# A four-part transformer block: the first attention unit's transposes and position biases moved into the end of the first feed-forward network, and raw weights loaded ahead of rows

## What is computed

```python
x = x + attn_a(layernorm(x))   # a stack: 512 -> 64, 4 layers of long convolution and MLP, -> 512 (+ bout)
x = x + ffn(layernorm(x))      # (silu(x Wg) * (x Wu)) Wd, inner size 1792
x = x + attn_b(layernorm(x))   # 32 query heads, 8 key heads of 128, rms norm of q and k
x = x + ffn(layernorm(x))      # the same weights again

# attn_b, per sequence
scores = einsum(q, k) / sqrt(128)
rel = pos[None, :] - pos[:, None]
bias = where(rel > 0, -1e30, slope[head] * rel)
out = softmax(scores + bias) @ v
return out @ Wo.T
```

## Time and profile before

| | us |
|---|---|
| median of 3 runs (lowest, highest) | 2420.01 (2417.81, 2420.99) |
| the profiled execution | 2419.45 |
| its span | 2418.1 |
| PE busy | 2356.0 (97%) |
| DVE, ACT, POOL busy | 1590.2, 1204.3, 838.7 |
| mean granted clock of PE | 0.987 |

### The profile page before, as it was taken

One profiled execution on the slowest core, in us unless ns is written; L12 is line 12 of the kernel. 1 busy time (PEld: TensorE's weight loads), 2 busy tenths in 40 slices (PEclk: granted clock), 3 DMA queues, 4 the chain that ended last, 5 costly groups with the idle time before them and its releaser, 6 DMA issues.

```text
span 2418.1 us, 41023 instructions
## 1 busy us (share of the span) xinstructions
PE 2356.0 (97%) x12810; PEld 2028.0 (84%) x12810; DVE 1590.2 (66%) x3897; ACT 1204.3 (50%) x3788; POOL 838.7 (35%) x1332
## 2 busy tenths in 40 slices
PE   6899999999999999999999999999999999999999
PEld 4577777888888888989989999899899978888887
DVE  7666565534267777777777777677777776565553
ACT  6433332333256666666666666666666662232211
POOL 4540343211034345545444455454444440011000
PEclk7899999999999999999999999999999999999999
DMA  4334558987831534545446345444462315565554
GB/s 130 114 112 177 204 207 277 346 337 278 337 123 57 231 125 164 214 151 176 176 177 233 125 164 214 151 173 179 177 233 92 114 38 216 196 217 184 192 190 157
DMA packets 92629, 444.87 MB, mean 184 GB/s; under 512 B 10168, under 2 KB 17336, under 8 KB 72704
## 3 DMA queue, kind: packets, MB, share of 16 engines
q1 hardware_dynamic: 91056, 440.78, 49.4%
q10 hardware_dynamic: 1360, 1.46, 0.2%
HBM read 342.59 MB, written 99.61 MB: 183 GB/s over the span
## 4 chain that ended last, share of the span: by engine, by line
PE 84%; DMA 6%; issue 3%; ACT 3%; DVE 2%; POOL 1%; SPq 1%; ACTq 0%; DVEq 0%; POOLq 0%
PE psum L800 71%; DMA stage<-in_wqkv 3%; PE psum L2666 3%; PE psum L2642 2%; DMA weff_s<-short_st 1%; PE psum L2660 1%; PE psum L1811 1%; ACT prob L2408 1%; PE psum L1832 1%; DMA weff_q<-q_parts 1%; PE psum L1802 1%; PE psum L1844 1%; PE psum L2661 1%; POOL srstd L1202 1%; POOL prob L2471 1%
## 5 line engine op out<-in xcount | busy, mean ns | idle before, releaser
L800 PE MATMUL psum<-qw,xs 128*128 128x384 f32 x2688 | 548.1, 346 | 1.1 <-DVE su L2498 0.7
L800 PEld LDWEIGHTS psum<-qw,xs 128*128 128x128 f32 x2688 | 456.8, 188 | 2.5 <-issue 1.3
L2471 POOL TENSOR_SCALAR prob<-prob,rsum 128x128 f32<-128x128 f32 (+1 forms) x512 | 231.4, 465 | 529.1 <-DVE rsum L2574 528.0
L2408 ACT ACTIVATE prob<-biased,nmax 128x256 f32<-128x256 f32 (+1 forms) x512 | 226.9, 445 | 112.5 <-DVE nmax L2564 109.2
L2582 DVE TENSOR_TENSOR oT_l<-psum,oT_h 128x512 fp32r<-128x512 f32 x128 | 88.4, 691 | 196.0 <-ACT oT_h L2420 195.9
L800 PE MATMUL psum<-wo_h,oT_h 128*128 128x512 f32 x512 | 208.2, 407 | 0.0
L800 PE MATMUL psum<-wo_l,oT_h 128*128 128x512 f32 x512 | 202.9, 396 | 0.0
L800 PE MATMUL psum<-wo_h,oT_l 128*128 128x512 f32 x512 | 202.5, 395 | 0.0
L2354 ACT ACTIVATE squares<-cc 128x128 f32<-128x128 f32 x512 | 154.4, 305 | 45.6 <-DVE cc L2501 28.5
L2432 POOL TENSOR_TENSOR rr<-ss,mneg_half 128x6 f32<-128x6 f32 (+1 forms) x128 | 150.3, 1174 | 10.6
L2415 ACT ACTIVATE pT_h<-psum 128x384 fp32r<-128x384 f32 x256 | 124.8, 488 | 57.3 <-PE psum L2666 55.1
(11 more groups left out here) (339 smaller groups left out, 5939.0 us busy)
## 6 DMA issues: line engine op xcount, KB each, us to landing
xs<-weff_x SPq DMA_DIRECT2D x62, 1792.0 KB, 8.2
wgu<-weff_gu SPq DMA_DIRECT2D x42, 1024.0 KB, 7.5
qw<-weff_q SPq DMA_DIRECT2D x56, 768.0 KB, 7.5
weff_q<-q_parts SPq DMA_DIRECT2D x84, 384.0 KB, 4.9
wD<-weff_dn SPq DMA_DIRECT2D x56, 512.0 KB, 4.6
wS<-weff_s SPq DMA_DIRECT2D x28, 1024.0 KB, 6.8
wdn<-weff_dn SPq DMA_DIRECT2D x42, 512.0 KB, 4.2
weff_gu<-wgu SPq DMA_DIRECT2D x14, 1024.0 KB, 4.4
```

The lines of the kernel that those rows point to most:

```text
L800: ins = pe.matmul(out_ap, stat[a], mov[b], start=start and n == 0, stop=stop and n == last)
L2408: act.activation(prob[:, b, lo:hi], biased[:, b % 2, lo:hi], ACT.Exp, bias=nmax[:, b, t:t + 1], scale=-1.0, accum_out=esum[:, b, t:t + 1]) ...
L2471: pool.tensor_scalar(prob[:, b, lo:hi], prob[:, b, lo:hi], rsum[:, b, t:t + 1], 1.0, ALU.mult, ALU.mult).then_inc(prob_done, 1)
```

## The change

1. Unit 0's transposes go between `up` 55 and the downs, with ACT's and DVE's parts behind them; they use banks 6, 0 and 7 instead of 5, 4 and 6. The mask and the biases stand on DVE between `dlo` 54 and `d` 55, `rel` at the end of POOL's phase-1 list. ACT runs one exp of a single column there, so that its table is loaded.
2. PE no longer passes `phase1_over`. Scores of heads 2 and 3 and the first product of unit 1 wait for the x additions that free their banks.
3. SP loads the rows of units 1 and 2 as soon as `up` 55 is done.
4. In unit 0 the split of the output weights moves inside the unit (ACT after `exp1` and after `pThi1`; POOL after the second and after the fourth `prob`).
5. In every unit SP's order is `sets0 sets1 set0` instead of `sets0 set0 sets1`, and in `set0` `qf` stands ahead of `lx`.
6. The places `rows` and `set1` are earlier on PE, ACT and DVE, which moves steps in units 2 to 5 only.
7. POOL's `bout` of blocks 1 to 3 waits for the four `frow` of block 0, in the planner and on the chip.

```diff
@@ stack_steps
-                o.add(("bout", s, t), "pool", 1.27, [("fold", 5, 0), ("row", s, t), ("w1", 0, t) if lead else ("xadd", 0, 1)], 6)
+                o.add(("bout", s, t), "pool", 1.27, [("fold", 5, 0), ("row", s, t), ("w1", 0, t) if lead else ("frow", 0, TPB - 1)], 6)
@@ behind order1 = first.ordered(patient=PATIENT)
+        end = NBLK * IC - 1
+        def follows(engine, key, *steps):
+            at = order1[engine].index(key) + 1
+            order1[engine][at:at] = steps
+        follows("pe", ("up", end, 1), ("qT", 0, 0), ("kT", 0, 0), ("qT", 0, 1))
+        follows("act", ("dhi", end, 0), ("qThi", 0, 0), ("kThi", 0, 0), ("qThi", 0, 1), ("table", 0, 0))
+        follows("dve", ("dlo", end - 1, 0), ("mask", 0, 0), *(("alibi", 0, hd) for hd in range(GRP)))
+        follows("dve", ("dlo", end, 0), ("kw", 0, 0), ("qTlo", 0, 0), ("kTlo", 0, 0), ("qTlo", 0, 1))
+        order1["pool"].append(("rel", 0, 0))
@@ pool_phase1, bout
                     wait_stack_row(pool, a, b)
+                    if a:
+                        pool.wait_ge(row_done, TPB)
@@ act_phase1
+                elif what == "table":
+                    act.wait_ge(s_out, 32 * IC)
+                    act.activation(table[:], mneg_half[:, 0:1], ACT.Exp)
@@ UNIT_STEPS
-            "pe": "sc0 sc1 sc2 qkv1 qkv7 sc3 qkv6 pT0 qkv5 pT1 qkv2 qkv4 at0 pT2 pT3 qkv3 rows outa0 set1 qT0 at1 outa1 kT0 qT1 "
+            "pe": "sc0 sc1 sc2 qkv1 qkv7 sc3 qkv6 pT0 qkv5 pT1 qkv2 qkv4 at0 rows pT2 pT3 qkv3 set1 outa0 qT0 at1 outa1 kT0 qT1 "
...
-            "dve": "bias0 bias1 rsum0 bias2 rsum1 bias3 wait0 rsum2 u2 u3 pTlo0 c22 pTlo1 c11 rsum3 set0 u4 c21 oTlo0 pTlo2 c12 "
-                   "rows pTlo3 wait1 oTlo1 set1 qTlo0 qTlo1 kTlo0 oadd0 vlo0 oadd1",
-            "act": "set0 exp0 exp1 exp2 prcopy0 pThi0 exp3 pThi1 sqr5 sqr2 oThi0 pThi2 sqr4 pThi3 rows wait1 sqr3 ksc0 set1 oThi1 "
+            "dve": "bias0 bias1 rsum0 bias2 rsum1 bias3 wait0 rsum2 u2 u3 pTlo0 c22 pTlo1 c11 rsum3 set0 u4 c21 rows oTlo0 pTlo2 c12 "
+                   "pTlo3 wait1 oTlo1 set1 qTlo0 qTlo1 kTlo0 oadd0 vlo0 oadd1",
+            "act": "set0 exp0 exp1 swo0 exp2 prcopy0 pThi0 exp3 pThi1 swo1 sqr5 sqr2 oThi0 rows pThi2 sqr4 pThi3 set1 wait1 sqr3 ksc0 oThi1 "
...
-            "sp": "sets0 set0 sets1",
+            "sp": "sets0 sets1 set0",
@@ besides
+            if engine == "act" and b == 0 and (where in ("swo0", "swo1") if g == 0 else where == "set0"):
+                steps += [("swo", g, int(where[-1]))] if g == 0 else [("swo", g, 0), ("swo", g, 1)]
+            if engine == "pool" and b == 0 and where in (("wait0", "sums") if g == 0 else ("set0", "wait0")):
+                steps.append(("swo", g, (("wait0", "sums") if g == 0 else ("set0", "wait0")).index(where)))
...
+                if g and later_g < KVH and b == 1:
+                    steps.append(("qf", later_g, 0))
                 if u + 3 < UNITS and u + 3 not in range(SEQS1, BATCH):
                     steps.append(("lx", u + 3, 0))
-                if g and later_g < KVH and b == 1:
-                    steps.append(("qf", later_g, 0))
@@ sp_phase2, behind the load of qkw
+            sp.wait_ge(xs_out, 32 * SEQS1)
+            sp.wait_ge(up_mm, NBLK * IC)
+            load_rows(1)
+            load_rows(2)
             phase1_over(sp)
@@ pe_projection, product 1
                 pe.wait_ge(kT_lo, a)
+                if a == 1:
+                    pe.wait_ge(fx_done, NT)
@@ new: where the transposes go, and what they wait for in unit 0
+        def across_bank(what, a, b):
+            if what == "kT":
+                return KV if a else AUX[1]
+            return QB[b] if a else (AUX[0], GATE)[b]
+        def pe_across(what, a, b):
+            if a == 0:
+                pe.wait_ge(c_done, len(SUMS2))
+                pe.wait_ge(gate_done, NBLK * IC)
...
@@ pe_phase2, sc
+                    if a == 0 and b >= DOWN:
+                        pe.wait_ge(fx_done, NT - TPB + b - DOWN + 1)
@@ the end of phase 1
-        for engine in (pe, act, dve, pool):
+        for engine in (act, dve, pool):
             phase1_over(engine)
...
-        pe.wait_ge(c_done, len(SUMS2))
         pe_phase2()
```

More of the change, by code:

```diff
@@ L1221, in pool_phase1 @@
                     pool_sequence(a)
+                elif what == "rel":
+                    pool_positions()
                 elif what == "bout":
@@ L1860, in pe_phase1 @@
                     pe_sequence(a, b)
+                elif what in ("kT", "qT"):
+                    pe_across(what, a, b)
                 else:
@@ L1955, in hybrid_block @@
         rsum = sb2("rsum", [P, GRP, STILES])
+        table = sb2("table", [P, 1])
         KV, QB, WO = 4, (5, 6), 7
@@ L2369, in act_projection, with act_across @@
                 ins.then_inc(k_sc, 1)
+        def act_across(what, a, b):
+            if what == "kT":
+                act.wait_ge(kT_mm, a + 1)
+                if a:
+                    act.wait_ge(sc_mm, GRP * a)
+                else:
+                    act.wait_ge(kw_mask_done, 2)
+                act.activation(kT[0], psum[:, across_bank(what, a, b), 0:SEQ], ACT.Copy, scale=kw[:]).then_inc(kT_hi, 1)
+            elif what == "qT":
+                act.wait_ge(qT_mm, STILES * a + b + 1)
+                if a:
+                    act.wait_ge(sc_mm, GRP * a)
+                act.activation(qT[0][:, :, b * P:(b + 1) * P], psum[:, across_bank(what, a, b), :].rearrange("p (h c) -> p h c", h=GRP),
+                               ACT.Copy).then_inc(qT_hi, 1)
         def act_phase2():
```

131 lines of the change are left out of this document (61 added, 70 removed).

## The result

The kernel after took 2392.28 us in the median of 4 runs (2387.74 to 2395.39). The kernel before took 2420.50 beside it (2417.81 to 2422.97). The ratio is 0.9882, 95% interval 0.9861 to 0.9903: faster, as forecast. The profiled execution took 2394.39 (span 2393.1), 25.0 us less than that of before, where the sum said 21.6.

The account below looks back on a forecast made before the run. PE, busy 97% of the span, was taken as the bound, so gains come only from its idle time and lower-clock matmuls. 13.2 + 3.8 + 1.6 + 1.7 - 0.4 + 1.7 = 21.6 us gave 2398.4, range 2393.5 to 2406.

Parts of the forecast that it names:

- Raw weights and saves: SP's list, units at places 2 and 4 of a group become like unit 11: gain 13.2 us, bounds 8 and 15.
- rival C: SP's raw load does not come earlier, or lands as late beside the row load: 2410 us; chance 0.04.
- The seam: Between the last down and unit 0's mark: PE's waits for all of phase 1 go, transposes move earlier; gain 3.8 us.
- unit 0: First attention unit: half-speed scores and the wait for rows go, 22.44 to 20.85 us; gain 1.6, bounds 0.6 and 2.5.
- Rows of sequences 6 and 7: Earlier steps gain 1.7 us in units 2 and 3; a wait of `outa0` loses 0.4 in units 4 and 5.
- `bout`: Ahead of PE's first gate, POOL's additions wait until the rows are written: gain 1.7 us, bounds 0 and 1.8.
- 2 us either way: Phase 1: allowance for the planner shifting the order of everything behind the changed `bout` dependence.
- the forecast's own spread: Whole kernel: about 2394 to 2403 us, since the parts' bounds, all low 2412 or all high 2391, won't fall together.
- A: Attention units: the copy is freed, but part of the stall stays; if half of 13.2 stays, 2405 us; chance 0.08.
- B: Phase 1's order shifts to the worse after the planner's new dependence, all else holding: 2402 to 2404 us; chance 0.08.
- D: Units at places 2 to 5: first save queues behind the row load, ACT's second copy waits; slower, 2458 us; chance 0.03.
- E: Raw load no earlier, and the seam's gains fail too, rows landing late and clock falling: 2418 us; chance 0.03.

Follow-up runs that it names:

- two other kernels: Kernel after with both SP-list edits undone, 2405.92 us; kernel after with the rows of sequences 6 and 7 at their old places, 2394.26 us.

## Why the prediction was right or wrong

**Raw weights and saves, 13.2:** right in sum (13.28 in the first pair, 13.3 in the means, 13.2 for the two edits alone). The step priced the raw load "about 12" in rival C and it was 10.7 when undone; the saves 2.0. What the prediction says at its start, that a gain can only come from idle time and from matmuls at the lower clock, left out a third source: 3.85 of the 13.28 are busy time at a granted clock of 1.00, which goes with the waits. The sum didn't need it, since it was made from lengths of units.

**The seam, 3.8, and unit 0, 1.6:** right against the trace they were read from (3.76 and 1.77). All steps showed: DVE's biases took 1.97 in their gap, the mark stands 0.70 behind the last down, the clock is 1.0, unit 0 is 20.67 against 20.85. But that trace was the mildest of three (of four with the kernel that has SP's edits alone, 30.2 from the last down to unit 1). The step took "heads 1 and 2 take 1.0 less" as the price of the lower clock and 0.6 as that of the rows; other executions of the kernel before take 1.6 and 3.1 us more at the same place, by both: the low clock reaches into the projection (1.8), and the wait for rows is 0.7 and 1.3 longer. With three traces of each this part gains 8.1 where the forecast has 6.4 (3.8 and 1.6, and the 1.0 of the transposes that it takes off elsewhere).

**Rows of sequences 6 and 7, +1.7 and -0.4:** 2.15 and -0.59, with the wait of the head outputs at 0.87 where 1.0 was forecast.

**`bout`, 1.7:** 1.8 or 2.55, by the clock at the gate; but with the long low clock part of it seems to be given back behind the gate. The prediction read the overlap rightly, but took 1.8 as its upper bound; with the short low clock it was 2.6. The planner's "2 us either way" can't be told from the spread: phase 1's weave differs by 2 to 4 us from trace to trace of one kernel.

**The sum:** 21.6 against 25.0 in the first pair and 22.5 in three of each. All runs of this study together have medians of 2417.8 (68 runs of the kernel before, 2412.06 to 2425.20) and 2394.4 (13 of after, 2387.74 to 2396.84), 23.4 apart. In the first set the medians are 28.2 apart: the kernel before was 2.7 above its own and the kernel after 2.1 below.

**The step that failed** is in "How the numbers follow": "the forecast's own spread is about 2394 to 2403". It was made of the bounds of the parts alone. Two things were missing. It had no term for what one execution differs from another in stretches that the change leaves alone (set-up 110.5 to 116.7 us, tail 452.3 to 453.7 in the kernel before), though the three times shown already differed by 3.2 us and the median of four runs carries part of that; and it priced the seam and unit 0, lower clock and wait for rows, from a single trace (6.4 against 8.1 in the means). The mechanisms of the parts were right. Which of the two put the first median 1.2 us below the range isn't shown, since three of its four runs have no trace; the median of all 13 runs, 2394.4, lies inside. A low end 3 to 4 us lower, near 2390, is what I estimate from these two. The forecast time itself was taken from a base of 2420.0, 2.2 above the median of the many runs; two of the three sets of the kernel after, 2396.08 and 2394.38, lie in the range.

**The rivals.** A (part of the stall stays): no, place 2 is 19.95 throughout. B (phase 1's order for the worse): not seen. POOL's order did change, but the stretch to the gate is 8.60 with either order, and the weave, 560.25 with the old and 561.46 with the new, differs no more than five traces of one order do. C: no, the load went out 27.6 us ahead of unit 10's mark where it was 7.7. D (slower, the first save behind the row load): no, the units at places 3 and 5 stay at 19.86 to 19.98. E: its piece, the rows landing late, is real when made (9 us), but didn't come with the change. The margin is thin, with waits of 0.24 and 0.49 in two other kernels.

## What to carry to other kernels

Read the lengths between marks that repeat, not only the list of waits: 11.2 us of waits were 13.2 us of units, and each undone edit came back at its place. Where a gap lowers the clock, price it from several executions, and look for the smallest part of the gap whose removal keeps the clock up: here either of two parts seems to do (one trace each), and each alone seemed to be worth 1 to 2 us while the two together were worth 6. A transfer that starts behind "everything is over" belongs beside the work that its target's last reader already allows; that one wait for rows alone cost 9 us (6.2 of waiting, and the restart at the lower clock), more than both gaps.

## What the hardware showed that I had not expected

The lower clock lasts unequally long in the same kernel. Behind the two gaps of the old seam the granted clock is under 1.00 from 688 to 692 us in one trace of the kernel before and from 688 to 698 in another, in windows of 2 us, although PE is busy without a pause from 693.58 on. At the first gate it is 114 to 119 us at a mean of 0.66 in one trace of the kernel after, where it fell behind an idle time of 1.46 us, and 114 to 124 at 0.52 in the next, where it fell two gaps later, in one of 1.91; there PE was busy 8.75 of those 10 us.

In the set-up, the first transposes of the rows come between 110.0 and 117.3 us, more than most edits of this change are worth. The mean granted clock over the first 90 us goes with it in part: 0.73 in the two latest traces (116.7 and 117.3), 0.85 in the earliest (110.0 to 110.6), but 0.86 with 114.4 in the third trace of the kernel after. So the clock isn't the whole of it, and what else differs is not shown.
